# A four-layer graph network on one core: a new order of the work of a turn, a third adjacency buffer, an earlier pause of the gather

## The chip, the cores and the metric

One core of a Trainium2 chip. The metric is the time on the device, in microseconds (us), of one execution of the whole program. The engines are TensorE (PE, with its weight loads PEld), VectorE (DVE), ScalarE (ACT), GpSimd (POOL) and SyncE (SP), which here only issues transfers. Each runs its own list of instructions in order, and they meet at semaphores.

## The reference

Sixteen graphs of 1024 nodes with 64 features (`x`), and for each a 0/1 adjacency matrix with about four ones in a row. Four layers, each with a residual:

```
def ln(x): return (x - mean(x)) / sqrt(var(x) + 1e-5)      # over the 64 features
# layer 0: normalized adjacency with self loops
h = max(ln(x), 0); A1 = adj + I; d = rowsum(A1) ** -0.5
x = x + relu((d[:, None] * A1 * d[None, :]) @ (h @ K0))
# layer 1: three powers of the normalized adjacency
h = max(ln(x), 0); g = A1 * d'[:, None] * d'[None, :]
x = x + concat([h, g h, g g h, g g g h]) @ W.T + b
# layer 2: neighbourhood quantiles
h = max(ln(x), 0)
#   rows with more than 10 neighbours lose every skip-th of them (both directions)
#   agg = 0.25 * q25 + 0.5 * q50 + 0.25 * q75 over the neighbours left and the node itself, per feature
x = x + mlp(h + agg) * mask            # 64 -> 128 -> relu -> 64
# layer 3
h = max(ln(x), 0)
x = x + adj @ (h @ W3) + b3
```

## The kernel before

A *batch* is one graph: 1024 nodes as 8 tiles (`T`) of 128 partitions. The program runs 20 *turns*, and in each it works on up to five batches at once, in the roles `n` (the next), `b` (this), `p` (the last), `c` (two back) and `d` (three back):

- `n`: its adjacency is loaded tile by tile into `adj_f` (`RING` = 2 buffers of 512 KB) and cast to f16 by ScalarE, which sums the degrees on the way (`cast`, L498); `degrees` (L1146) makes the scales; norm0 is computed and split into two bf16 parts (`split`, L1020) for layer 0.
- `b`: TensorE transposes the adjacency (`transpose_adjacency`, L596), then come layer 0 (`h0`, product `lin0`), norm1, and layer 1 as three rounds of an adjacency product `turned_half` (L622), a copy by ScalarE, a product back `turned_back` (L645) and `propagate` on VectorE (L1252): `lin1`, `v1`, `v2`, `v3`, ended by `layer1_out` (L1258). Beside this it prepares the quantiles: nodes with 8 or more in their row are *wide*; `place_of` (PE, L657) and `select_wide` (DVE, L1157) give each a place, `compact` (L674) gathers their rows, `widest` (L1133) and `wide_drops` (L1168) choose what is dropped, `row_keys` (PE, L710, a product per tile) and `row_list` (DVE, L1211, a top 8) list the neighbours of every row, `wide_lists` and `flag_crowds` mend what is special. `row_numbers` (L1215) turns the lists into row numbers for the gather, and `store_h2` (SP) stores the normalized rows to a table in HBM.
- `p`: `weights` (L1220) makes the quantile weights from the lists. It runs at the start of the turn after its lists.
- between the turns: the `gather` (POOL, L400) takes 72 indirect transfers of 128 rows for a batch. It starts when the row numbers are ready and runs on into the next turn. It has pauses, `abreast` (L423), in which it waits for a product or a transposition of the batch behind: after 14 transfers for `lin0`, then for `select`, `lin1`, `v1`, `v2`. For the last batch there is none.
- `c`: VectorE sorts the gathered slots (`sort_1` to `sort_6`, L1036 to L1065), merges the wide ones (`merge_first`, `merge_rest`, `wide_sum`), weighs and sums (`narrow_weighing`, `narrow_sum`, `aggregate`, L1270); TensorE transposes the aggregate and runs the two-layer MLP (`hidden_rows`, L734, ScalarE's `hidden`, L516, `mlp_rows`, L804); `add_mlp` (L1277); then norm3 and layer 3 (`h3`, `lin3`).
- `d`: `add_layer3` (L1264) adds layer 3, and SP stores the result (`store_result`); behind that store on SP stand the load of the next `x` and of tiles 2 to 7 of the next adjacency.

What sets the order: each engine has its turn written out by hand, in the loops `for turn in turns` (SP L326, POOL L448, ScalarE L521, TensorE L813, VectorE L1283). The PSUM banks are used in turn: `ps_tr` has two for transpositions and adjacency products, `ps_key` two for the key products, `ps_prod` and `ps_misc` one each. The tables `TR`, `KEY`, `MISC`, `PROD`, `PARTS` (L79 to L88) number their uses in the order of the turn, and each user waits until the use before its own (two before, where there are two banks) is free. A normalization is four steps: sums on VectorE (`norm_begin`), squares and a root on ScalarE (`norm_spread`), scales on VectorE (`norm_scale`), the result on ScalarE (`norm_apply`).

Of the kernel before, what the change touches and what calls it, by code (L numbers as in the profile page):

```python
# [48 lines left out]
def gnn_stack(nc, x_in, adj, nodemask, w_l0, w_l1, b_l1, w1, b1, w2, b2, w_l3, b_l3, out):  # L49
# [6 lines left out]
    T = N // P  # L56
# [5 lines left out]
    RING = 2  # L62
# [12 lines left out]
    for i in range(-1, B + 3):  # L75
        turns.append({role: (i + ahead if 0 <= i + ahead < B else None)
                      for role, ahead in (("n", 1), ("b", 0), ("p", -1), ("c", -2), ("d", -3))})
# [3 lines left out]
                     ("b", "v1.1"), ("b", "v2.0"), ("b", "v2.1"), ("c", "agg.0"), ("c", "agg.1"), ("b", "v3.0"),  # L81
                     ("b", "v3.1"), ("c", "h3.0"), ("c", "h3.1")])
    KEY = numbered(turns, [("b", "place"), ("b", "compact"), ("b", "pairs"), ("b", "row0"), ("b", "row1"),
                           ("b", "cross"), ("b", "row2"), ("b", "over")] + [("b", f"row{t}") for t in range(3, T)])
# [6 lines left out]
    with ctx:  # L91
# [255 lines left out]
        def _(pool):  # L347
# [52 lines left out]
            def gather(g):  # L400
# [26 lines left out]
                for t in range(T):  # L427
                    if t == 2:
                        abreast(prod_full, PROD.get(("lin0", g + 1), 0) + 1)
# [24 lines left out]
        def _(act):  # L454
# [66 lines left out]
            for turn in turns:  # L521
# [7 lines left out]
                if b is not None:  # L529
                    for t in range(T):  # L530
                        adjacency_columns(b, t)
                    halves("h0", b, columns_t[:, :])
                casts(0, 1)
                if b is not None:
                    norm_spread("norm1", b, h_rows[:, :, 0:C])
# [5 lines left out]
                casts(2, 6)  # L541
                if b is not None:
                    half_of("v1", b, 0, columns_t[:, :])
                casts(6, 7)
                if b is not None:
                    half_of("v1", b, 1, columns_t[:, :])
                casts(7, 8)
                if n is not None:
                    degree_roots(n)
                if b is not None:  # L550
                    halves("v2", b, columns_t[:, :])
                if c is not None:
                    halves("agg", c, columns_t[0:C, :])
                    hidden(c, 0)
                if b is not None:
                    half_of("v3", b, 0, columns_t[:, :])
                if c is not None:
                    hidden(c, 1)
                if b is not None:
                    half_of("v3", b, 1, columns_t[:, :])  # L560
                if b is not None:
                    norm_spread("norm2", b, tiles(h2[b % 2]))
                if n is not None:
                    norm_spread("norm0", n, y)
                if b is not None:
                    norm_apply("norm2", b, tiles(h2[b % 2]), h2_ready)
                    own_rows(b)
                if c is not None:
# [9 lines left out]
        def _(pe):  # L578
# [234 lines left out]
            for turn in turns:  # L813
                b, c = [turn[role] for role in "bc"]
                if b is not None:
                    place_of(b)
# [25 lines left out]
                if c is not None:  # L842
                    spread_wide(c)
                if b is not None:
# [5 lines left out]
                if c is not None:  # L850
                    transpose_features("agg", c, lambda t: agg[:, t, :], C, agg_ready)
                if b is not None:
                    own_weights("v3", b, DEPTH - 3)
# [540 lines left out]
```

## Time and profile before

| | us |
|---|---|
| median of 3 runs | 2063.82 |
| lowest and highest of them | 2052.77, 2066.84 |
| span of the profiled execution | 2057.6 |
| busy in it: VectorE | 1476.0 (72%) |
| TensorE | 1414.9 (69%) |
| POOL | 1277.9 (62%) |
| ScalarE | 811.7 (39%) |

The profiled execution is known by its span, first to last instruction; it lies 6.2 us (0.3%) under the median of the runs. Times in the profile count from the start of the span. Busy shares are averages over the whole of it: at either end stand stretches in which only some of the roles have a batch. A wait line says which engine waited, at which line and tile, and which instruction released it.

### The profile page before, as it was taken

What the parts mean: (1) busy time and instruction counts of PE and PEld (TensorE: products, weight loads), DVE (VectorE), ACT (ScalarE), POOL (GpSimd) and SP (SyncE); (2) the same over time, 40 slices, a digit from 0 to 9 for tenths busy, and PEclk for the clock granted to TensorE, in tenths of its full rate; (3) what the DMA queues carried; (4) which work ended last, traced back from release to release, by engine and by line L of the source; (5) the groups of instructions that cost most, each with busy time, mean ns of one, the idle gap of its engine ahead of it and who ended that gap; (6) DMA issues with size and microseconds to landing.
All of it is one profiled execution on the core that took longest, in us unless ns stands there. A gap on an engine that the chain in (4) does not pass through costs nothing.

```text
span 2057.6 us, 25735 instructions
## 1 busy us (share of the span) xinstructions
PE 1414.9 (69%) x8885; PEld 820.3 (40%) x8997; DVE 1476.0 (72%) x2315; ACT 811.7 (39%) x2292; POOL 1277.9 (62%) x1196
## 2 busy tenths in 40 slices
PE   1778776777868677786967676787867678683314
PEld 0444434444434443443444444444444344342102
DVE  1162886878778686867868697877868687887563
ACT  4443435435343534425253444424353443412101
POOL 2017787766757576575757667574767667577720
PEclk9898878877888888888888888788888788886555
DMA  3113334333233333332333333323333332213210
GB/s 118 62 37 88 55 82 56 86 48 79 36 63 75 57 83 49 90 25 61 75 55 83 50 90 50 79 37 60 77 57 81 48 90 30 23 25 33 25 14 5
DMA packets 106621, 120.22 MB, mean 58 GB/s; under 512 B 71486, under 2 KB 71614, under 8 KB 106430
## 3 DMA queue, kind: packets, MB, share of 16 engines
q0 software_dynamic: 36864, 37.82, 18.5%
q1 hardware_dynamic: 69566, 79.98, 12.4%
q8 instruction: 103, 1.69, 0.3%
q14 instruction: 88, 0.72, 0.1%
HBM read 109.27 MB, written 8.45 MB: 57 GB/s over the span
## 4 chain that ended last, share of the span: by engine, by line
DVE 40%; PE 32%; POOL 11%; issue 9%; ACT 6%; DMA 1%; DVEq 1%; POOLq 0%; SPq 0%; ACTq 0%
PE ps_tr L630 11%; POOL slots L407 10%; DVE lists L1212 6%; PE ps_tr L638 5%; DVE slots L1031 4%; DVE slots L1032 4%; PE ps_prod L649 3%; DVE slots L1114 3%; PE ps_misc L809 2%; PE ps_tr L619 2%; ACT z_mid L494 2%; DVE stat_norm L1007 2%; PE ps_misc L738 2%; ACT adj_t L465 2%; DVE slots L1039 2%
## 5 line engine op out<-in xcount | busy, mean ns | idle before, releaser
L407 POOL DMA_INDIRECT slots<-h_rows,row_no x1152 | 1266.1, 1099 | 687.3 <-issue 341.4
L465 ACT ACTIVATE columns_t<-ps_tr 128x512 f32<-128x512 f32 (+1 forms) x192 | 112.9, 595 | 689.8 <-PE ps_tr L638 518.9
L630 PE MATMUL ps_tr<-adj_t,y_mid 128*128 128x512 bf16 x960 | 259.8, 414 | 24.5 <-DVEq L1025 17.7
L1212 DVE MAX8 lists<-ps_key 128x8 f16<-128x1024 f32 x128 | 157.8, 1232 | 72.7 <-PE ps_key L719 60.7
L503 ACT ACTIVATE adj_n<-adj_f 128x1024 f16<-128x1024 f32 x128 | 134.6, 1052 | 155.9 <-PE ps_key L683 79.3
L630 PEld LDWEIGHTS ps_tr<-adj_t,y_mid 128*128 128x128 bf16 x1024 | 98.6, 105 | 225.5 <-issue 153.6
L630 PE MATMUL ps_tr<-adj_t,z_mid 128*128 128x512 bf16 x240 | 86.7, 512 | 115.2 <-DVEq L1025 114.5
L638 PE MATMUL ps_tr<-adj_t,low 128*64 128x512 bf16 x1024 | 142.3, 402 | 0.0
L484 ACT ACTIVATE h<-x,stat_norm 128x64 f32<-128x64 f32 x256 | 85.1, 334 | 126.7 <-DVEq L1009 126.7
L715 PE MATMUL ps_key<-select_t,dropped 128*128 128x512 bf16 x224 | 90.9, 483 | 63.5 <-DVEq L1144 55.7
L465 ACT ACTIVATE adj_t<-ps_tr 128x1024 bf16<-128x1024 f16 x128 | 119.2, 1032 | 30.6 <-PE ps_tr L602 30.6
L619 PE MATMUL ps_tr<-h_t,w_l_sb 65*128 65x512 f32 x192 | 127.8, 801 | 3.4 <-ACT columns_t L465 3.4
L1031 DVE TENSOR_TENSOR slots<-slots 128x2560 f32<-128x2560 f32 (+1 forms) x64 | 116.8, 1825 | 5.3
L1032 DVE TENSOR_TENSOR slots<-slots 128x2560 f32<-128x2560 f32 (+1 forms) x64 | 116.3, 1817 | 0.0
L494 ACT ACTIVATE h<-x,stat_norm 128x64 f32<-128x64 f32 x256 | 88.2, 427 | 49.0 <-DVEq L1018 49.0
L602 PE MATMUL ps_tr<-ident_h,adj_n 128*128 128x128 f16 x1024 | 78.0, 224 | 42.3 <-ACT adj_t L465 42.3
L1254 DVE TENSOR_TENSOR y_mid<-ps_prod,scales 128x512 f32<-128x512 f32 x48 | 33.2, 691 | 95.1 <-PE ps_prod L649 69.6
L719 PE MATMUL ps_key<-key_diag,adj_t 128*128 128x128 f16 x1024 | 100.7, 256 | 0.0
L649 PEld LDWEIGHTS ps_prod<-both_ident,columns_t 128*128 128x128 f32 x768 | 94.5, 196 | 15.3 <-issue 15.3
L612 PE MATMUL ps_tr<-ident_f,h 128*65 128x128 f32 x128 | 31.1, 423 | 92.7 <-ACT h L494 92.7
L649 PE MATMUL ps_prod<-both_ident,columns_t 128*128 128x64 f32 x768 | 94.2, 277 | 0.0
L719 PEld LDWEIGHTS ps_key<-key_diag,adj_t 128*128 128x128 bf16 x1024 | 83.4, 119 | 23.6 <-issue 14.9
(211 smaller groups left out, 2604.2 us busy)
## 6 DMA issues: line engine op xcount, KB each, us to landing
adj_f<-in_adj SPq DMA_DIRECT2D x128, 512.0 KB, 4.5
slots<-h_rows,row_no POOLq DMA_INDIRECT x1152, 3.3
x<-in_x SPq DMA_DIRECT2D x16, 256.0 KB
h_rows<-h SPq DMA_DIRECT2D x16, 256.0 KB, 4.7
out<-x SPq DMA_DIRECT2D x16, 256.0 KB, 2.7
xc<-in_L_gnn_W SPq DMA_DIRECT2D x1, 64.0 KB
w_sb<-in_L_gnn_W SPq DMA_DIRECT2D x2, 32.0 KB
h_rows<-zeros SPq DMA_DIRECT2D x2, 32.0 KB, 1.5
```

The lines of the kernel that those rows point to most:

```text
L407: pool.indirect_dma_start(out=slots[:, slot_of(par, s), t * C:(t + 1) * C], out_offset=None, in_=table[par][:, :], in_offset=bass.Indirect ...
L465: act.activation(dst, view, ACT.Copy, scale=scale).then_inc(tr_free, 1)
L494: last = act.activation(to[:, t, :], x[g % 4][:, t * C:(t + 1) * C], ACT.Relu, bias=shift[:, t:t + 1], scale=rstd[:, t:t + 1])
L503: act.activation(adj_n[:, t * N:(t + 1) * N], adj_f[:, k % RING, :], ACT.Copy, accum_out=deg[:, t:t + 1]).then_inc(cast_done, 1)
L619: nc.tensor.matmul(tr_bank(f"{name}.{i}", g)[:, :], w_l1_sb[:, part, :], h1_t[:, i * HALF:(i + 1) * HALF], start=True, stop=False)
L630: nc.tensor.matmul(dst[:, :], top_halves(pair_of)[:, j, :], adj_t[g % 3][:, columns[j]], start=(j == 0 and not begun), stop=False)
L638: last = nc.tensor.matmul(dst[rows, :], low_of[:, j, 0:C], adj_t[g % 3][:, columns[j]], start=False, stop=(j >= T - 2))
L649: last = nc.tensor.matmul(ps_prod[:, t * C:(t + 1) * C], columns_t[:, t * P:(t + 1) * P], weights[:, :], start=start, stop=(start or t == ...
L719: last = nc.tensor.matmul(dst[:, j * P:(j + 1) * P], adj_t[g % 3][:, j * N + t * P:j * N + (t + 1) * P], key_diag[:, j, :], start=False, s ...
L1031: st.done(v.tensor_tensor(low_to, first, second, ALU.min))
L1032: step(v.tensor_tensor(high_to, first, second, ALU.max))
L1212: step(v.max(out=lists[:, t * SLOTS:(t + 1) * SLOTS], in_=read_key(f"row{t}", g)))
```

## The change

Nothing is computed otherwise; what is moved is the place of the work in a turn.

- `RING` goes from 2 to 3: three adjacency buffers.
- POOL: the first pause of the gather, after 14 transfers, waits for the last adjacency transposition of the batch behind (`adj7`) and no longer for its `lin0` product.
- `degrees` moves behind the row lists; `place_of` and `select_wide` are done for the next batch at the end of a turn, ahead of layer 3, and not for this batch at its start. `weights` moves from the start of the next turn to the end of the same one; the role `p` is gone.
- VectorE: the sorts open the turn, `add_layer3` follows `sort_2`; `widest` and `wide_drops` stand ahead of the result of `v1`, the first two lists ahead of that of `v2`, `wide_lists` and the third behind it, and the narrow sums and `aggregate` move from ahead of `v2` to behind it, ahead of `layer1_out`. The sums of norm0 stand ahead of the degrees.
- TensorE: row keys 0 and 1 ahead of `v2`, `cross` and row key 2 ahead of `v3`; the transposition of the aggregate and the hidden layer move behind `v3`, with the other row keys among them.
- ScalarE: the spread of norm1 ahead of the first cast; six casts have other places; the hidden layer behind the spread of norm2, the spread of norm0 behind norm2's result and the copy of its rows.

```diff
@@ -61,3 +61,3 @@
     EPS = 1e-5
-    RING = 2
+    RING = 3
     COLS = T + 2
@@ -80,6 +80,7 @@
                   + [("b", "h0.0"), ("b", "h0.1"), ("b", "select"), ("b", "h1.0"), ("b", "h1.1"), ("b", "v1.0"),
-                     ("b", "v1.1"), ("b", "v2.0"), ("b", "v2.1"), ("c", "agg.0"), ("c", "agg.1"), ("b", "v3.0"),
-                     ("b", "v3.1"), ("c", "h3.0"), ("c", "h3.1")])
-    KEY = numbered(turns, [("b", "place"), ("b", "compact"), ("b", "pairs"), ("b", "row0"), ("b", "row1"),
-                           ("b", "cross"), ("b", "row2"), ("b", "over")] + [("b", f"row{t}") for t in range(3, T)])
+                     ("b", "v1.1"), ("b", "v2.0"), ("b", "v2.1"), ("b", "v3.0"), ("b", "v3.1"), ("c", "agg.0"),
+                     ("c", "agg.1"), ("c", "h3.0"), ("c", "h3.1")])
+    KEY = numbered(turns, [("b", "compact"), ("b", "pairs"), ("b", "row0"), ("b", "row1"), ("b", "cross"),
+                           ("b", "row2"), ("b", "over")] + [("b", f"row{t}") for t in range(3, T)]
+                   + [("n", "place")])
     MISC = numbered(turns, [("c", "spread"), ("c", "hid.0"), ("c", "hid.1"), ("c", "mlp")])
@@ -428,3 +429,3 @@
                     if t == 2:
-                        abreast(prod_full, PROD.get(("lin0", g + 1), 0) + 1)
+                        abreast(tr_full, TR.get((f"adj{T - 1}", g + 1), 0) + 1)
                     if t == 4:
@@ -532,5 +533,5 @@
                     halves("h0", b, columns_t[:, :])
+                    norm_spread("norm1", b, h_rows[:, :, 0:C])
                 casts(0, 1)
                 if b is not None:
-                    norm_spread("norm1", b, h_rows[:, :, 0:C])
                     from_tr("select", b, select_t[b % 3][:, :], tr_bank("select", b)[:, :].bitcast(bf16), PAD)
@@ -540,9 +541,9 @@
                     halves("h1", b, h1_t[:, :])
-                casts(2, 6)
+                casts(2, 4)
                 if b is not None:
                     half_of("v1", b, 0, columns_t[:, :])
-                casts(6, 7)
+                casts(4, 5)
                 if b is not None:
                     half_of("v1", b, 1, columns_t[:, :])
-                casts(7, 8)
+                casts(5, 8)
                 if n is not None:
@@ -551,18 +552,15 @@
                     halves("v2", b, columns_t[:, :])
+                    halves("v3", b, columns_t[:, :])
                 if c is not None:
                     halves("agg", c, columns_t[0:C, :])
-                    hidden(c, 0)
                 if b is not None:
-                    half_of("v3", b, 0, columns_t[:, :])
+                    norm_spread("norm2", b, tiles(h2[b % 2]))
                 if c is not None:
+                    hidden(c, 0)
                     hidden(c, 1)
                 if b is not None:
-                    half_of("v3", b, 1, columns_t[:, :])
-                if b is not None:
-                    norm_spread("norm2", b, tiles(h2[b % 2]))
-                if n is not None:
-                    norm_spread("norm0", n, y)
-                if b is not None:
                     norm_apply("norm2", b, tiles(h2[b % 2]), h2_ready)
                     own_rows(b)
+                if n is not None:
+                    norm_spread("norm0", n, y)
                 if c is not None:
@@ -813,5 +811,4 @@
             for turn in turns:
-                b, c = [turn[role] for role in "bc"]
+                n, b, c = [turn[role] for role in "nbc"]
                 if b is not None:
-                    place_of(b)
                     transpose_adjacency(b)
@@ -841,5 +838,5 @@
                     turned_back("v1", "v1", b, both_ident, False)
-                if c is not None:
-                    spread_wide(c)
-                if b is not None:
+                    pe.wait_ge(dropped_ready, b + 1)
+                    row_keys(b, 0)
+                    row_keys(b, 1)
                     own_weights("v2", b, DEPTH - 2)
@@ -850,5 +847,15 @@
                 if c is not None:
-                    transpose_features("agg", c, lambda t: agg[:, t, :], C, agg_ready)
+                    spread_wide(c)
                 if b is not None:
+                    cross_drops(b)
                     own_weights("v3", b, DEPTH - 3)
+                    row_keys(b, 2)
+                    for i in range(2):
+                        turned_half("v3", b, i, y_mid, low, begun=True)
+                    loop_rows("v3", b)
+                    turned_back("v3", "v3", b, both_ident, False)
+                if c is not None:
+                    transpose_features("agg", c, lambda t: agg[:, t, :], C, agg_ready)
+                if b is not None:
+                    count_over(b)
                 if c is not None:
@@ -856,3 +863,3 @@
                 if b is not None:
-                    turned_half("v3", b, 0, y_mid, low, begun=True)
+                    row_keys(b, 3)
                 if c is not None:
@@ -860,12 +867,3 @@
                 if b is not None:
-                    turned_half("v3", b, 1, y_mid, low, begun=True)
-                    loop_rows("v3", b)
-                    pe.wait_ge(dropped_ready, b + 1)
-                    row_keys(b, 0)
-                    row_keys(b, 1)
-                    turned_back("v3", "v3", b, both_ident, False)
-                    cross_drops(b)
-                    row_keys(b, 2)
-                    count_over(b)
-                    row_keys(b, 3)
+                    row_keys(b, 4)
                 if c is not None:
@@ -873,6 +871,6 @@
                 if b is not None:
-                    row_keys(b, 4)
-                    row_keys(b, 5)
-                    row_keys(b, 6)
-                    row_keys(b, 7)
+                    for t in range(5, T):
+                        row_keys(b, t)
+                if n is not None:
+                    place_of(n)
                 if c is not None:
@@ -1283,3 +1281,3 @@
             for turn in turns:
-                n, b, p, c, d = [turn[role] for role in "nbpcd"]
+                n, b, c, d = [turn[role] for role in "nbcd"]
                 st.restart()
@@ -1291,8 +1289,2 @@
 
-                if p is not None:
-                    weights(p)
-                if b is not None:
-                    select_wide(b)
-                if d is not None:
-                    add_layer3(d)
                 if c is not None:
@@ -1304,3 +1296,7 @@
                     sort_2(c)
+                if d is not None:
+                    add_layer3(d)
+                if c is not None:
                     sort_3(c)
+                    sort_4(c)
                 if b is not None:
@@ -1309,8 +1305,7 @@
                 if c is not None:
-                    sort_4(c)
+                    sort_5(c)
                 if b is not None:
-                    norm_scale("norm1", b, s_root)
                     wide_keys(b)
+                    norm_scale("norm1", b, s_root)
                 if c is not None:
-                    sort_5(c)
                     sort_6(c)
@@ -1321,2 +1316,5 @@
                     propagate(b, "lin1")
+                    widest(listed[:, :], key_w[:, :], key_left)
+                    wide_drops(b)
+                    propagate(b, "v1")
                 if c is not None:
@@ -1324,4 +1322,7 @@
                     wide_sum(c)
+                row_lists(0, 2)
                 if b is not None:
-                    propagate(b, "v1")
+                    propagate(b, "v2")
+                    wide_lists(b)
+                row_lists(2, 3)
                 if c is not None:
@@ -1331,11 +1332,6 @@
                 if b is not None:
-                    propagate(b, "v2")
-                    widest(listed[:, :], key_w[:, :], key_left)
-                    wide_drops(b)
-                if n is not None:
-                    degrees(n)
-                row_lists(0, 2)
-                if b is not None:
                     layer1_out(b)
                     norm_begin("norm2", b)
+                    flag_crowds(b)
+                row_lists(3, 4)
                 if n is not None:
@@ -1344,9 +1340,4 @@
                 if b is not None:
-                    wide_lists(b)
-                row_lists(2, 3)
-                if b is not None:
-                    flag_crowds(b)
-                row_lists(3, 4)
-                if b is not None:
                     norm_scale("norm2", b)
+                row_lists(4, 5)
                 if c is not None:
@@ -1354,5 +1345,9 @@
                     norm_begin("norm3", c)
+                row_lists(5, 8)
+                if b is not None:
+                    row_numbers(b)
                 if n is not None:
+                    degrees(n)
                     norm_scale("norm0", n, d0[n % 2])
-                row_lists(4, 8)
+                    select_wide(n)
                 if c is not None:
@@ -1360,3 +1355,3 @@
                 if b is not None:
-                    row_numbers(b)
+                    weights(b)
                 if c is not None:
```

## Rows read from the trace of the kernel before

**Rows 1.** VectorE's timeline (start, duration), row numbers and first sort.

```profile
141.44 0.20 DVE L1217 TENSOR_SCALAR row_no<-row_no_f 128x81 int32<-128x81 f32 x1
...
234.26 0.20 DVE L1217 TENSOR_SCALAR row_no<-row_no_f 128x81 int32<-128x81 f32 x1
...
241.68 2.83 DVE L1039 TENSOR_TENSOR slots<-slots 128x2560 f32<-128x2560 f32 x1 [0.40 <-DMA slots<-h_rows,row_no]
...
1865.22 0.22 DVE L1217 TENSOR_SCALAR row_no<-row_no_f 128x81 int32<-128x81 f32 x1
```

**Rows 2.** Waits (total, times, longest), one turn, 950.9 to 1067.4.

```profile
POOL slots L407 <- PE ps_prod L649: 10.4, 1, 10.4
...
PE ps_key L707 <- DVEq L1200: 4.2, 1, 4.2
...
DVE place L1158 <- PE ps_key L663: 3.6, 1, 3.6
...
DVE lists L1212 <- PE ps_key L719: 2.6, 2, 1.8
DVE y_mid L1254 <- PE ps_prod L649: 2.4, 1, 2.4
DVE z_mid L1279 <- PE ps_misc L809: 2.4, 1, 2.4
...
DVE z_mid L1023 <- ACT z_mid L494: 2.3, 1, 2.3
```

**Rows 3.** VectorE's timeline of one turn; in brackets the idle time before.

```profile
940.79 0.17 DVE L1221 TENSOR_SCALAR scale<-wide 128x8 f32<-128x8 bf16 x1 [0.25 <-DVE low L1024]
...
950.94 2.83 DVE L1039 TENSOR_TENSOR slots<-slots 128x2560 f32<-128x2560 f32 x1 [0.34 <-DVE x L1266]
...
965.06 0.69 DVE L1248 SCALAR_TENSOR_TENSOR y_mid<-ps_prod,scales 128x512 f32<-128x512 f32 x1
...
972.11 1.49 DVE L1055 TENSOR_TENSOR slots<-slots 128x1280 f32<-128x1280 f32 x1
...
985.90 0.69 DVE L1254 TENSOR_TENSOR y_mid<-ps_prod,scales 128x512 f32<-128x512 f32 x1 [1.03 <-issue]
```

**Rows 4.** ScalarE's waits in the first 45 us (total, times, longest).

```profile
ACT adj_n L503 <- DMA adj_f<-in_adj: 9.7, 6, 2.8
ACT y_mid L484 <- DVEq L1009: 2.0, 1, 2.0
```

**Rows 5.** TensorE's timeline of the same turn.

```profile
962.71 2.00 PE L649 MATMUL ps_prod<-w_l_sb,columns_t 128*128 128x64 f32 x16
...
979.87 3.68 PE L834 MATMUL ps_prod<-w_l_sb,h_t 65*128 65x64 f32 x16 [0.68 <-ACT h_t L465]
...
988.74 3.19 PE L630 MATMUL ps_tr<-adj_t,y_mid 128*128 128x512 bf16 x7 [1.68 <-DVEq L1025]
```

**Rows 6.** ScalarE's timeline of the same turn.

```profile
968.71 1.06 ACT L503 ACTIVATE adj_n<-adj_f 128x1024 f16<-128x1024 f32 x1 [5.29 <-PE ps_key L683]
...
1030.00 0.35 ACT L484 ACTIVATE h<-x,stat_norm 128x64 f32<-128x64 f32 x1 [6.95 <-DVEq L1009]
```

**Rows 7.** TensorE's timeline of turn 0, first seven products of v1.

```profile
86.33 2.87 PE L630 MATMUL ps_tr<-adj_t,y_mid 128*128 128x512 bf16 x7 [0.22 <-issue]
```

**Rows 8.** TensorE by stretches: length, busy (instructions), granted clock, DMA share, GB/s.

```profile
977.20:983.50 6.30, 5.57 (x25) 0.50 0.55 170
...
1036.50:1040.60 4.10, 4.10 (x19) 0.50 0.16 24
```

**Rows 9.** TensorE's timeline of the last turn: hidden layer and MLP.

```profile
2026.04 2.04 PE L738 MATMUL ps_misc<-columns_t,w_sb 64*128 64x512 f32 x2 [0.87 <-ACT merged L518]
...
2029.40 3.68 PE L809 MATMUL ps_misc<-w_sb,merged 128*128 128x64 f32 x16
```

**Rows 10.** POOL's timeline: first gathers of batches 0 and 1.

```profile
142.63 1.59 POOL L407 DMA_INDIRECT slots<-h_rows,row_no  x1 [127.11 <-DVEq L1218]
...
236.15 0.94 POOL L407 DMA_INDIRECT slots<-h_rows,row_no  x1 [1.98 <-DMA h_rows<-h]
```

More of the change, by code:

```diff
@@ L551, in _ @@
                     halves("v2", b, columns_t[:, :])
+                    halves("v3", b, columns_t[:, :])
                 if c is not None:
                     halves("agg", c, columns_t[0:C, :])
-                    hidden(c, 0)
-                if b is not None:
-                    half_of("v3", b, 0, columns_t[:, :])
-                if c is not None:
-                    hidden(c, 1)
-                if b is not None:
-                    half_of("v3", b, 1, columns_t[:, :])
                 if b is not None:
                     norm_spread("norm2", b, tiles(h2[b % 2]))
-                if n is not None:
-                    norm_spread("norm0", n, y)
+                if c is not None:
+                    hidden(c, 0)
+                    hidden(c, 1)
                 if b is not None:
@@ L841, in _ @@
                     turned_back("v1", "v1", b, both_ident, False)
-                if c is not None:
-                    spread_wide(c)
-                if b is not None:
+                    pe.wait_ge(dropped_ready, b + 1)
+                    row_keys(b, 0)
+                    row_keys(b, 1)
                     own_weights("v2", b, DEPTH - 2)
@@ L850, in _ @@
                 if c is not None:
+                    spread_wide(c)
+                if b is not None:
+                    cross_drops(b)
+                    own_weights("v3", b, DEPTH - 3)
+                    row_keys(b, 2)
[4 more added lines that the diff above has]
+                if c is not None:
                     transpose_features("agg", c, lambda t: agg[:, t, :], C, agg_ready)
                 if b is not None:
-                    own_weights("v3", b, DEPTH - 3)
+                    count_over(b)
                 if c is not None:
@@ L1304, in _ @@
                     sort_2(c)
+                if d is not None:
+                    add_layer3(d)
+                if c is not None:
                     sort_3(c)
+                    sort_4(c)
                 if b is not None:
@@ L1309, in _ @@
                 if c is not None:
-                    sort_4(c)
+                    sort_5(c)
                 if b is not None:
+                    wide_keys(b)
                     norm_scale("norm1", b, s_root)
-                    wide_keys(b)
                 if c is not None:
-                    sort_5(c)
                     sort_6(c)
```

## The prediction

> **What bounds the kernel now.** I read three things in this order: the start of each turn on VectorE, the waits within one turn, and the timelines of VectorE, TensorE and ScalarE beside each other. The row numbers of batch 1 are ready at 234.46 us and those of batch 15 at 1865.44 [rows 1]; between them lie 14 turns, so a turn takes 116.5. The head up to the first sort (241.68) and the tail behind the last row numbers (2057.6 - 1865.4 = 192.2) are the rest. In the turn that starts at 940.79 no engine is full: VectorE waits 3.6 for the places, 2.6 for row keys, 2.4 for the v1 product, 2.4 for the MLP, 2.3 for z, 1.0 on "issue", and about 2.5 in small pieces, some 16.8 with the places at this turn's own 3.9 [rows 2, 3]. So its work is 116.7 - 16.8 = 99.9 a turn. The gather is not behind: POOL waits 10.4 for the lin0 product in a turn, and it ends before the next row numbers [rows 2]. The bound is the ping-pong between VectorE, TensorE and ScalarE. The change removes no work in a turn; what counts is which waits are left.
>
> **The pause and the third buffer.** The last adjacency transposition ends about 10 us before the lin0 product, so up to 10.4 us of pause go [rows 2]. Those gathers then run beside the sorts. Nobody waits for them in a steady turn, so I take 0 for the turn; the price for POOL is in the rivals. Three buffers hide ScalarE's waits for adjacency; in the first turn these are 9.7 in six [rows 4]. Between 0 and -9.7 I take -3, since two transfers in flight already follow each other at 2.6 us.
>
> **A steady turn, wait by wait** (0 is the restart behind the last split).
> 1. Places and weights: select moves ahead of the split, behind the place product, which now stands on TensorE behind the row keys: its wait of 3.6 to 3.9 goes. The 3.6 of weights and 1.7 of selection move into the stretch in which ScalarE normalizes; the 2.3 wait for z goes too, the one for y stays at 0.5.
> 2. lin0 product: it ends at 964.71 (962.71 + 2.00 [rows 5]), 23.9 behind the restart. h3 now starts 0.5 later against the restart, so 24.2. Work ahead of its reader: sorts 1 to 3, 14.1 (950.94 to 965.06), sort 4, four passes of 1.49, and the output of layer 3, 1.0 [rows 3]: 21.1. **New wait 3.1.** The result store and, behind it on SP, the loads of x and of tiles 3 to 7 come 2.6 later; the first cast comes at 30, so nobody waits. ScalarE's spread for norm1 no longer stands behind the cast, which in the trace waits 5.3 for the compaction and starts 1.2 behind the mean [rows 6].
> 3. lin1: in the trace from the mean (967.5) to its end (979.87 + 3.68) 16.05 [rows 5], now 14.85. VectorE's work between (sort 5, wide keys, scale, sort 6, merge) is 11.3. **New wait 3.5** (it covers the 1.03 of "issue" [rows 3]).
> 4. v1: its own weights are done 3.6 behind lin1 (983.55 to 988.74 less the idle 1.68 [rows 5]), 1.3 behind the parts, so TensorE does not idle. With idle 1.68 the first seven matmuls took 3.19, with 0.22 2.87 in turn 0 [rows 5, 7], and the whole of v1 9.5 instead of 10.5. Against this stand 9.1 of list and drop work. **New wait 1.7** (was 2.4).
> 5. v2 and v3: two row keys (1.9) and own weights (1.95) stand in front of v2, cross and row 2 in front of v3. VectorE has 11.4 of merging, wide sum and two lists against 3.85 + 8.2 behind the parts: 0 (slack 0.8). The narrow sum covers v3.
> 6. Here the change costs. The aggregate now ends after v3, so TensorE idles 4.6 (v3 done to aggregate), about as long as the 4.2 before the count in the trace [rows 2], behind which its row keys and the MLP ran at 1.2 GHz: granted clock 0.50 [rows 8]. Behind the aggregate: ScalarE first does layer 1's spread (mean at +2.75, 3.0 long as at 1030.00 [rows 6]), then hidden 0 (0.7), TensorE hidden 1 2.04, row key 4 1.9, MLP 0.5 + 3.68 [rows 9]: together 14.65. VectorE's own work meanwhile: layer 1 out 2.75, flag, row 3, sums for norm0, scale, row 4: 7.4. **New wait 7.25**, in place of 2.6 and 2.4.
> 7. Row key 7 0.6, restart 0.25.
>
> Sum: 3.1 + 3.5 + 1.7 + 7.25 + 0.6 + 0.5 + 0.25 = 16.9, so a turn is 116.8, I take 116.9 against 116.5: **nothing is gained in a steady turn**. At full clock in step 6 (row key and hidden 0.95 and 1.05, MLP 2.4) the chain is 10.9, row key 7 costs nothing, and a turn is 113.3.
>
> **The head.** Row numbers of batch 0 were at 141.64. Buffers -3; the sums of norm0 stand ahead of the degrees, so ScalarE's 2.0 wait goes [rows 4]; the spread ahead of the cast -1.4; list and drop work (9.1) and three lists leave the chain behind v2 for TensorE's time, less two waits of 1 for row keys, -10. Together 125.4. The gather then takes as long as before (142.6 to 234.2 [rows 10]), to 218.0, and the sort starts 5 to 7.5 behind it: 224.5 instead of 241.68. Turn 1 alone would end at 221: row numbers 86.6 behind the first (92.8 before, -11.4, +5.2 since ScalarE's transposed columns now wait behind its norm0), and 8.6. In the first full turn TensorE is ahead, and the 3.1 of step 2 drop out. Head: -17.2 - 3 = **-20**.
>
> **The tail.** Output of layer 3 for batch 14 stood in the wait for the last gather, now behind sort 2: +1.0. Nothing else in it moves.
>
> **Sum.** 224.5 + 14 x 116.9 - 11.0 (row numbers to first sort) - 3.1 + 192.2 + 1.0 = 2040 against the profiled 2057.6. That span is 6.2 below the median of 2063.82 and inside the runs' 2052.77 to 2066.84, so 2046.
>
> **Rivals.**
> - *Full clock behind the aggregate.* TensorE is busy almost all of the 14.6, and a turn is 113.3: 14 x 3.6 = 50 less, 1996. Against it: from 977.2 to 983.5, busy for 5.6 of 6.3, the clock stays at 0.50, and in the MLP of the trace, with row keys on both sides, too [rows 8].
>  The Trainium skill (TensorE: Matmul & The Clock Gate, "What's actually happening") says that what warms the clock up is sustained busy time and not a number of matmuls; by that rule this rival's 1996 would come true, and the two stretches just named disagree.
> - *Low clock on into h3 and lin0 (slower).* Place: TensorE's wait between row key 7 and h3, 6.95 before, about 10 now, since weights and selection stand ahead of z's split. Price: h3's second half 2.9 and its product 1.9 at 1.2 GHz, straight into the wait for lin0, which is open. A turn is then 121.7 and the kernel 2046 + 67 = 2113. It decides from 1.3 us a turn on (18 of head gain over 14 turns). Against it: in the tail h3 follows 11.0 of idling and costs about 4.6 for its first half, as in every turn.
> - *The head does not move*, because the gather or the landing holds the first sort, or ScalarE's order eats the gain: then 2064, no change.
> - *POOL becomes the bound.* Gathers beside sorts 1 and 2 take about 2.5 instead of 0.94. Ten of those are 15 us, in place of the 10.4 pause: POOL then needs 106 a turn, still below 116.9, so this alone changes nothing; it only cuts off gains below 106.
>
> **Chances.** My forecast (a turn of 115.5 to 118.5, its own range 2026 to 2068) 0.52, of which 0.20 below 2043 and 0.32 within 1%; full or partly full clock (1990 to 2020) 0.23; low clock further on, or another slip of over 2.7 us a turn, 0.15, 0.04 of it within 1%; unmoved head 0.10, half of it within 1%, half beyond. Within 1% is what a measurement of this kernel can tell from no change: 2043 to 2084. So faster 0.43, same 0.41, slower 0.16. The range leaves out the ends of both rivals: 1994 to 2085.
>
> **What would show it.** Right: first sort at 220 to 228; a period of 116 to 118; VectorE's longest wait in a turn at the MLP or row 4 (together 7), then lin1 and lin0 with 3 to 4; no wait for places; POOL's pause under 2 us; clock 0.50 from the aggregate to row key 6. Wrong: no low clock there (period 113), a lin0 wait above 6 (period 120 and more), a POOL that starts its gather late, or the first sort still near 241.

## The result, and the profile after

| | before | after |
|---|---|---|
| median of 4 runs | 2062.26 | 2082.26 |
| lowest and highest | 2052.77, 2066.84 | 2080.52, 2083.51 |
| profiled execution | 2057.6 | 2078.8 |
| VectorE busy in it | 1476.0 | 1475.7 |
| TensorE busy | 1414.9 | 1461.2 |
| POOL busy | 1277.9 | 1364.0 |

The ratio to the kernel before is 1.0106, 95% interval 1.0078 to 1.0134: the change costs 1%, 20 us. The forecast was 2046, a gain of 18. The range up to 2085 holds 2082 near its end, and not by the forecast's own working.

VectorE's timeline (start, duration) gives the stages, as [rows 1] did:

```profile
122.67 0.20 DVE L1215 TENSOR_SCALAR row_no<-row_no_f 128x81 int32<-128x81 f32 x1
...
211.31 0.20 DVE L1215 TENSOR_SCALAR row_no<-row_no_f 128x81 int32<-128x81 f32 x1
...
225.45 2.83 DVE L1037 TENSOR_TENSOR slots<-slots 128x2560 f32<-128x2560 f32 x1 [5.32 <-DMA slots<-h_rows,row_no]
...
1884.67 0.20 DVE L1215 TENSOR_SCALAR row_no<-row_no_f 128x81 int32<-128x81 f32 x1
```

The row numbers of batch 1 come at 211.51 and not at 234.46: the head gives back 23 (16 at the first sort, which now waits 5.3 for the last gather and waited 0.4 [rows 1]). Between batches 1 and 15 lie 1673.4 and not 1631.0, so a turn takes 119.5 on average where it took 116.5: 42 lost. The tail is 193.9 (2078.8 - 1884.87) against 192.2. -23 + 42 + 2 = +21, the difference of the spans.

VectorE's waits (total, times, longest) in one turn, 1179.5 to 1299.2, against [rows 2]:

```profile
DVE y_mid L1246 <- PE ps_prod L647: 5.7, 1, 5.7
DVE lists L1210 <- PE ps_key L717: 4.8, 2, 3.2
DVE y_mid L1252 <- PE ps_prod L831: 3.6, 1, 3.6
DVE z_mid L1277 <- PE ps_misc L807: 2.9, 1, 2.9
DVE y_mid L1252 <- PE ps_prod L647: 2.0, 1, 2.0
```

The places are gone from the list, as is the wait for z. First stands the wait for the lin0 product (L1246), with 5.7 where 3.1 was forecast.

TensorE's timeline of the same turn (h3 at 1177.77 and 1181.27, h0 from 1196.34, lin0 at 1204.23, then the chain behind the aggregate), then its stretches (length, busy with instructions, granted clock, DMA share, GB/s):

```profile
1168.96 0.19 PE L659 MATMUL ps_key<-wide,prefix 128*128 128x8 bf16 x1 [2.57 <-DVEq L1150]
...
1177.77 3.57 PE L628 MATMUL ps_tr<-adj_t,z_mid 128*128 128x512 bf16 x8 [8.43 <-DVEq L1023]
1181.27 1.66 PE L636 MATMUL ps_tr<-adj_t,low_z 128*64 128x512 bf16 x8
...
1196.34 0.31 PE L632 MATMUL ps_tr<-ident_b,y_mid 128*128 128x128 bf16 x1 [1.51 <-ACT adj_t L466]
...
1197.19 2.86 PE L628 MATMUL ps_tr<-adj_t,y_mid 128*128 128x512 bf16 x7
...
1204.23 2.00 PE L647 MATMUL ps_prod<-w_l_sb,columns_t 128*128 128x64 f32 x16
...
1266.41 1.89 PE L610 MATMUL ps_tr<-ident_f,z_mid 128*64 128x128 f32 x8 [4.47 <-DVEq L1273]
...
1277.15 3.67 PE L807 MATMUL ps_misc<-w_sb,merged 128*128 128x64 f32 x16
```

```profile
1177.90:1187.60 9.70, 9.65 (x47) 0.76 0.12 14
1195.60:1206.60 11.00, 10.26 (x66) 0.84 0.32 48
...
1266.40:1276.60 10.20, 9.37 (x34) 0.50 0.38 26
1276.60:1280.70 4.10, 4.10 (x19) 0.50 0.95 20
```

And what answers to the first two stretches in the kernel before, its h3 and its h0 to lin0:

```profile
1170.42 3.57 PE L630 MATMUL ps_tr<-adj_t,z_mid 128*128 128x512 bf16 x8 [6.59 <-DVEq L1025]
1173.92 1.16 PE L638 MATMUL ps_tr<-adj_t,low_z 128*64 128x512 bf16 x8
...
1188.63 0.22 PE L634 MATMUL ps_tr<-ident_b,y_mid 128*128 128x128 bf16 x1 [1.44 <-ACT adj_t L465]
...
1189.07 1.67 PE L630 MATMUL ps_tr<-adj_t,y_mid 128*128 128x512 bf16 x7
```

```profile
1170.30:1180.10 9.80, 9.63 (x53) 0.80 0.21 26
1188.20:1197.20 9.00, 8.57 (x66) 1.00 0.04 7
```

TensorE starts h3 after an idle 8.43, with another 2.57 shortly before it (before: 6.59 in one). Its clock over h3 is 0.76 instead of 0.80, and over h0 and lin0 0.84 instead of 1.00: the first seven products of h0 take 2.86, in the kernel before 1.67. The last two stretches are step 6: the whole chain behind the aggregate stays at 0.50, at 1.2 GHz, as forecast.

POOL's waits in that turn (total, times, longest), and its group of gathers in the page (busy, mean ns, idle before):

```profile
POOL slots L408 <- DVEq L1216: 11.5, 1, 11.5
```

```profile
L408 POOL DMA_INDIRECT slots<-h_rows,row_no x1152 | 1352.2, 1174 | 621.1 <-issue 339.8
```

The pause of 10.4 [rows 2] is gone and POOL now waits 11.5 for the row numbers: it is not behind.

### The profile page after: what moved, and what is told of

Read it like the earlier page. It is cut to its first block, busy times and chain, and to the rows that moved or that the text cites. A ratio compares the mean times of both kernels' runs of the same rounds, so it can differ in the third digit from the quotient of the medians.

```text
span 2078.8 us, 25753 instructions
## 1 busy us (share of the span) xinstructions
PE 1461.2 (70%) x8888; PEld 848.0 (41%) x8997; DVE 1475.7 (71%) x2315; ACT 806.0 (39%) x2292; POOL 1364.0 (66%) x1196
## 4 chain that ended last, share of the span: by engine, by line
PE 38%; DVE 32%; ACT 13%; POOL 8%; issue 7%; DMA 1%; DVEq 0%; POOLq 0%; SPq 0%; ACTq 0%
PE ps_tr L628 10%; POOL slots L408 7%; DVE lists L1210 5%; ACT adj_t L466 5%; PE ps_tr L636 5%; PE ps_prod L647 4%; ACT h L485 3%; DVE slots L1112 3%; PE ps_tr L610 3%; PE ps_tr L617 3%; PE ps_prod L831 3%; PE ps_misc L807 3%; ACT h L495 2%; PE ps_misc L736 2%; DVE slots L1124 1%
## 5 line engine op out<-in xcount | busy, mean ns | idle before, releaser
L408 POOL DMA_INDIRECT slots<-h_rows,row_no x1152 | 1352.2, 1174 | 621.1 <-issue 339.8
L628 PE MATMUL ps_tr<-adj_t,y_mid 128*128 128x512 bf16 x992 | 276.3, 425 | 16.3 <-DVEq L1023 12.8
L628 PEld LDWEIGHTS ps_tr<-adj_t,y_mid 128*128 128x128 bf16 x1024 | 104.2, 108 | 204.2 <-issue 135.6
L636 PE MATMUL ps_tr<-adj_t,low 128*64 128x512 bf16 x1024 | 136.6, 389 | 0.0
L466 ACT ACTIVATE adj_t<-ps_tr 128x1024 bf16<-128x1024 f16 x128 | 119.9, 1032 | 29.7 <-PE ps_tr L600 29.7
L617 PE MATMUL ps_tr<-h_t,w_l_sb 65*128 65x512 f32 x192 | 121.6, 767 | 0.0
L485 ACT ACTIVATE h<-x,stat_norm 128x64 f32<-128x64 f32 x256 | 85.4, 335 | 86.1 <-DVEq L1007 86.1
L717 PE MATMUL ps_key<-key_diag,adj_t 128*128 128x128 f16 x1024 | 105.9, 265 | 0.0
L628 PEld LDWEIGHTS ps_tr<-adj_t,z_mid 128*128 128x128 bf16 x256 | 27.7, 118 | 187.3 <-issue 176.1
L717 PEld LDWEIGHTS ps_key<-key_diag,adj_t 128*128 128x128 bf16 x1024 | 87.9, 124 | 25.2 <-issue 17.9
L600 PEld LDWEIGHTS ps_tr<-ident_h,adj_n 128*128 128x128 f16 x1024 | 66.2, 104 | 58.7 <-issue 57.4
```

The lines of the kernel that those rows point to most:

```text
L408: pool.indirect_dma_start(out=slots[:, slot_of(par, s), t * C:(t + 1) * C], out_offset=None, in_=table[par][:, :], in_offset=bass.Indirect ...
L466: act.activation(dst, view, ACT.Copy, scale=scale).then_inc(tr_free, 1)
L485: last = act.activation(scratch[:, t, :], x[g % 4][:, t * C:(t + 1) * C], ACT.Square, bias=less_mean[:, t:t + 1], accum_out=var[:, t:t + 1])
L600: last = nc.tensor.transpose(view[:, j, :], adj_n[:, t * N + j * P:t * N + (j + 1) * P], ident_h[:, :])
L617: nc.tensor.matmul(tr_bank(f"{name}.{i}", g)[:, :], w_l1_sb[:, part, :], h1_t[:, i * HALF:(i + 1) * HALF], start=True, stop=False)
L628: nc.tensor.matmul(dst[:, :], top_halves(pair_of)[:, j, :], adj_t[g % 3][:, columns[j]], start=(j == 0 and not begun), stop=False)
```

## The experiments

*Theory A*: the turn is longer because TensorE's clock is low in h3 and h0, just ahead of the one wait that is open there. *Theory B*: without its pause the gather runs beside h3, h0 and lin0 and slows them. Each run was taken in three rounds beside the kernel before; the period T is the distance of the row numbers of batches 1 and 15 over 14, as above. The last column is read from TensorE's timelines: in 13 turns h3 and h0 both run, and it counts those in which h0, from its first product to the start of lin0, took 7.6 us or more, where the others take 6.3 to 6.5. Most kernels carry a helper which gives TensorE products whose result the next true product overwrites:

```diff
+            def keep_busy(name, g, times):
+                tr_turn(name, g)
+                for k in range(times):
+                    nc.tensor.matmul(tr_bank(name, g)[:, :], ones, adj_t[g % 3][:, 0:HALF], start=True, stop=True)
```

| run | built on | median | ratio to before [95%] | T | slow h0, of 13 |
|---|---|---|---|---|---|
| before | | 2062.26 | | 116.5 | 1 |
| after | before | 2082.26 | 1.0106 [1.0078, 1.0134] | 119.5 | 12 |
| busy_h3 | after | 2043.67 | 0.9917 [0.9889, 0.9945] | 116.65 | 1 |
| busy_agg | after | 2079.99 | 1.0094 [1.0061, 1.0127] | 119.2 | 11 |
| pause_lin0 | after | 2087.24 | 1.0121 [1.0092, 1.0150] | 119.8 | 13 |
| late_weights | after | 2048.99 | 0.9930 [0.9906, 0.9955] | 117.2 | 4 |
| hidden_first | after | 2068.89 | 1.0042 [1.0021, 1.0063] | 118.3 | 8 |
| chain_warm | busy_agg | 2001.21 | 0.9719 [0.9679, 0.9758] | 113.9 | 3 |
| late_chain | chain_warm | 1984.58 | 0.9641 [0.9602, 0.9680] | 112.75 | 8 |
| select_in_wait | late_chain | 1981.68 | 0.9602 [0.9571, 0.9634] | 112.5 | 9 |
| two_buffers | after | 2087.49 | 1.0143 [1.0107, 1.0178] | 119.55 | 13 |
| before_busy | before | 2050.54 | 0.9949 [0.9926, 0.9973] | 116.45 | 0 |

**busy_h3**: the two idle stretches ahead of h3 are filled.

```diff
+                if c is not None:
+                    keep_busy("h3.0", c, 10)
                 if n is not None:
                     place_of(n)
                 if c is not None:
+                    keep_busy("h3.0", c, 30)
                     turned_half("h3", c, 0, z_mid, low_z)
```

> The changed kernel, with 10 products of 128x512 bf16 more before the place product and 30 more behind it, into the bank that the first half of h3 overwrites; all else as in the changed kernel. Theory A (the longer wait of TensorE ahead of h3 lowers its clock in h3 and h0, and that makes the lin0 product 2.6 us later than I had it): the granted clock from h3 to lin0 is near 1.00 in place of 0.77 and 0.84, VectorE's wait for lin0 falls from 5.7 to about 2.5 us, a turn from 119.5 to 116.3, and the median from 2082 to about 2037. Theory B (lin0 is late for another reason: the gathers that now run beside the transpositions and h0, or ScalarE's copies): the clock rises, but the wait stays above 5 and the time at 2082.

TensorE's timeline of a turn (h3's first half, h0's first half), then VectorE's at the reader of lin0:

```profile
921.99 1.89 PE L628 MATMUL ps_tr<-adj_t,z_mid 128*128 128x512 bf16 x8 [1.72 <-DVEq L1031]
...
938.65 1.67 PE L628 MATMUL ps_tr<-adj_t,y_mid 128*128 128x512 bf16 x7
```

```profile
946.61 0.69 DVE L1254 SCALAR_TENSOR_TENSOR y_mid<-ps_prod,scales 128x512 f32<-128x512 f32 x1 [1.52 <-PE ps_prod L647]
```

The first products of h3 take 1.89 instead of 3.57, those of h0 1.67, and VectorE waits 1.52 for lin0 instead of 5.7. Nothing but the fillers was added, and 38.6 are gone. Theory A is shown: the low clock there is worth more than the whole loss. It is worth more because the fillers also raise the clock in h3, which was low in the kernel before too (0.80).

**pause_lin0**: the gather's pause as before.

```diff
-                        abreast(tr_full, TR.get((f"adj{T - 1}", g + 1), 0) + 1)
+                        abreast(prod_full, PROD.get(("lin0", g + 1), 0) + 1)
```

> The changed kernel, with the gather's first pause back at the lin0 product. Theory A: POOL's pause is some 10 us a turn again, POOL still ends ahead of the next row numbers, and the time stays at 2082 within 5. Theory B (gathers beside the transpositions and h0 make lin0 late): VectorE's wait for lin0 falls by 2 to 3 us, a turn to 117, the median to about 2047.

POOL's waits over the span, then VectorE's wait for lin0 in the turn 1067 to 1186.7:

```profile
POOL slots L408 <- PE ps_prod L647: 154.3, 17, 12.4
```

```profile
DVE y_mid L1246 <- PE ps_prod L647: 5.7, 1, 5.7
```

The pause is back and the wait is 5.7 as in the change: theory B falls. The earlier pause is neither the loss nor a gain beyond the noise (the intervals of this and of the change overlap).

**busy_agg**: the wait for the aggregate is filled.

```diff
                 if c is not None:
+                    keep_busy("agg.0", c, 18)
                     transpose_features("agg", c, lambda t: agg[:, t, :], C, agg_ready)
```

> The changed kernel, with 18 products of 128x512 bf16 more in TensorE's 4.5 us wait for the aggregate, into the bank that the aggregate's transposition overwrites. If the low clock behind that wait is what the MLP chain costs, the chain from the aggregate to the MLP falls from 14.5 to about 11 us, VectorE's waits for row 3, row 4 and the MLP from 7.7 to about 4.1, a turn to 116, the median to about 2032. If VectorE then only waits at the next place (lin0), or the clock falls in the chain all the same, the time stays within 10 us of 2082.

TensorE's timeline behind the aggregate of one turn:

```profile
1142.80 1.03 PE L610 MATMUL ps_tr<-ident_f,z_mid 128*64 128x128 f32 x8 [0.57 <-DVEq L1279]
...
1149.10 2.04 PE L736 MATMUL ps_misc<-columns_t,w_sb 64*128 64x512 f32 x2 [2.84 <-ACT merged L519]
```

The transposition runs at full clock (1.03 for eight, 1.89 after). Then TensorE waits 2.84 for ScalarE's `hidden`, which stands behind the spread of norm2, and the second half of the hidden layer and the MLP take 2.04 and 3.67 again. The fill was in the right place, but a second gap behind it undoes it.

**late_weights**: `weights` and `select_wide` go back from the end of the turn to the start of the next, on VectorE alone.

```diff
                 st.restart()
...
+                if p is not None:
+                    weights(p)
+                if b is not None:
+                    select_wide(b)
...
                     norm_scale("norm0", n, d0[n % 2])
-                    select_wide(n)
...
-                if b is not None:
-                    weights(b)
                 if c is not None:
                     dve.wait_ge(z_ready, c + 1)
```

> The changed kernel, with the weights and the selection on VectorE back at the start of the next turn, behind the two splits (5.3 us). Theory A: the split of z, and with it h3, comes 2.9 us earlier behind the row numbers, TensorE's wait ahead of h3 falls from 11 to 8 us, the two steps lie in the wait for lin0 (5.7), which shrinks to under 1; a turn falls by 1.8 us to 117.7, the median to about 2057. If the end of the turn is bound by ScalarE's two normalizations instead, the time stays at 2082 or grows by up to 2.4 us a turn (2115).

TensorE's timeline of a turn and of h0 in the next one, and VectorE's at lin0 of the first:

```profile
923.43 3.57 PE L628 MATMUL ps_tr<-adj_t,z_mid 128*128 128x512 bf16 x8 [5.88 <-DVEq L1023]
...
942.71 2.69 PE L628 MATMUL ps_tr<-adj_t,y_mid 128*128 128x512 bf16 x7
...
1058.63 1.67 PE L628 MATMUL ps_tr<-adj_t,y_mid 128*128 128x512 bf16 x7
```

```profile
952.37 0.69 DVE L1246 SCALAR_TENSOR_TENSOR y_mid<-ps_prod,scales 128x512 f32<-128x512 f32 x1
```

In the first of these turns the clock in h3 and h0 is as low as after (3.57, 2.69); h0 is that slow in 4 of 13 turns, and in the other 9 it is at full clock, as in the second. VectorE waits for lin0 in neither kind, since it has 5.3 more of other work ahead of its reader. In the changed kernel the two steps stood where VectorE would otherwise wait for z and y; there 2.9 and 1.2 of waiting come back, while the 5.7 in front of lin0 goes. The turn is 2.3 shorter.

**chain_warm** fills the wait for the aggregate and takes the gap behind it away: `hidden(c, 0)` on ScalarE ahead of norm2's spread.

```diff
 # TensorE
+                    keep_busy("agg.0", c, 18)
 # ScalarE
+                if c is not None:
+                    hidden(c, 0)
                 if b is not None:
                     norm_spread("norm2", b, tiles(h2[b % 2]))
                 if c is not None:
-                    hidden(c, 0)
                     hidden(c, 1)
```

> The kernel of busy_agg (18 products more in TensorE's wait for the aggregate), and on ScalarE the copy of hidden 0 ahead of layer 1's spread in place of behind it. Theory A (the chain behind the aggregate is held first by ScalarE's spread, 3 us, and then by the low clock that the wait for it brings): no wait of 2.8 us between hidden 0 and hidden 1, full clock up to the MLP, VectorE's waits for row 3, row 4 and the MLP from 7.7 to 2 to 3 us, a turn from 119.5 to 114.5, the median from 2080 to about 2012. Theory B (other waits take over, or the clock falls anyway): above 2065.

TensorE's timeline of a turn (the hidden layer and the MLP), its stretches (the chain, then h3, then h0), and VectorE at lin0:

```profile
994.38 1.09 PE L737 MATMUL ps_misc<-columns_t,w_sb 64*128 64x512 f32 x2 [0.29 <-issue]
...
1000.12 2.26 PE L808 MATMUL ps_misc<-w_sb,merged 128*128 128x64 f32 x16
```

```profile
994.40:1002.40 8.00, 6.78 (x43) 0.96 0.20 27
906.00:915.00 9.00, 8.50 (x42) 0.80 0.12 13
923.00:932.00 9.00, 7.88 (x61) 1.00 0.33 53
```

```profile
932.53 0.69 DVE L1253 SCALAR_TENSOR_TENSOR y_mid<-ps_prod,scales 128x512 f32<-128x512 f32 x1 [3.33 <-PE ps_prod L648]
```

The chain runs at 0.96, with hidden products of 1.09 and 1.12 and an MLP of 2.26. h3's first half is still slow (3.45, behind an idle 8.46), but h0 runs at full clock here and in 10 of 13 turns, and the wait for lin0 is 3.33, near the forecast's 3.1. So an idle stretch of 8.4 ahead of h3 alone does not slow h0. Nor is the gain over busy_agg the chain's alone: averaged over the 13 turns the wait for lin0 falls from 5.4 to 3.9.

**late_chain** is chain_warm with late_weights' edit.

```diff
+                    weights(p)
...
+                    select_wide(b)
...
-                    select_wide(n)
...
-                    weights(b)
```

> chain_warm and late_weights together. If the two places are independent, a turn is 117.3 less 5, about 112.3, and the median about 1981; if the shorter chain only opens the wait for lin0 or lin1 again, between 2010 and 2049.

T is 112.75. The two gains don't add up (113.9 less 2.3 would be 111.6); the likely reason, not tested alone, is that the wait for lin0, into which the moved work goes, was down to 3.9 on average already.

**two_buffers**: the change with two adjacency buffers.

```diff
-    RING = 3
+    RING = 2
```

> The changed kernel with two adjacency buffers in place of three. By my steps the third buffer is worth 3 us in the first turn and nothing later: the median is about 2085, the row numbers of batch 0 near 126 in place of 122.7. If the casts, which stand ahead of ScalarE's copies of v1, wait for adjacency then, a turn grows by 1 to 3 us and the median to 2096 or more.

ScalarE's waits for adjacency in the first 45 us (total, times, longest), with two buffers and after:

```profile
ACT adj_n L504 <- DMA adj_f<-in_adj: 9.2, 6, 2.4
```

```profile
ACT adj_n L504 <- DMA adj_f<-in_adj: 3.5, 4, 1.2
```

The row numbers of batch 0 come at 129.7 and not at 122.9, and the period is that of the change (119.55). But busy_h3 and pause_lin0, which have three buffers and differ from the change only behind that point, have them at 126.7 and 126.1. So the third buffer is worth 3 to 7, in the head, and the medians (2087.49, and 2087.24 for pause_lin0) don't tell even this from noise.

**before_busy**: 28 fillers ahead of h3 in the kernel before.

```diff
                 if c is not None:
+                    keep_busy("h3.0", c, 28)
                     turned_half("h3", c, 0, z_mid, low_z)
```

> The kernel before, with 28 products of 128x512 bf16 more in TensorE's wait of 7 us ahead of h3. They raise the clock in h3 there too, and the lin0 product comes some 2 us earlier; but VectorE reads it behind sort 3 and does not wait for it there, so the time stays at that of the kernel before, within 6 us. If the clock of h3 counts by itself, wherever VectorE waits, it falls by 14 x 2, to about 2035.

TensorE's timeline, h3's first half of one turn:

```profile
932.92 1.89 PE L630 MATMUL ps_tr<-adj_t,z_mid 128*128 128x512 bf16 x8
```

h3 is at full clock, and the period 116.45 against 116.50: VectorE waits for lin0 in none of the 13 turns there. The median is nevertheless 0.5% below, 9 us where at most 6 was expected. The profiled execution is the slowest of this kernel's ten (2057.19, the others 2042.15 to 2054.23), so its period doesn't speak for the median. Whether the higher clock gave these 9 us stays open.

**hidden_first** is the move of ScalarE's in chain_warm without any filler.

```diff
+                if c is not None:
+                    hidden(c, 0)
                 if b is not None:
                     norm_spread("norm2", b, tiles(h2[b % 2]))
                 if c is not None:
-                    hidden(c, 0)
                     hidden(c, 1)
```

> The changed kernel with ScalarE's copy of hidden 0 ahead of layer 1's spread, and no products more. Theory A (the order and the low clock each hold the chain behind the aggregate; taking away one leaves the other): at low clock row key 3 keeps TensorE until 6 us behind the aggregate anyway, hidden 1 starts 0.5 us earlier, a turn falls from 119.5 to about 119, the median to about 2075. Theory B (the order alone is what chain_warm gained): about 2005 to 2020.

The turn is 118.3: the order alone takes off 1.2, the fill alone (busy_agg) 0.3, both together 5.6. With the order alone h0 is slow in 8 of 13 turns and not in 12, and 1.6 of the 5.6 is the shorter wait for lin0 (5.5 on average in the change, 3.9 in chain_warm), so the chain's own share is smaller than 5.6. The lin0 wait stays open, in the waits over the span (total, times, longest):

```profile
DVE y_mid L1247 <- PE ps_prod L648: 96.0, 15, 15.7
```

**select_in_wait** keeps `select_wide` at the end of the turn, behind norm3's scale, where VectorE waits for z.

```diff
-                if b is not None:
-                    select_wide(b)
...
                 if c is not None:
                     norm_scale("norm3", c)
+                if n is not None:
+                    select_wide(n)
```

> late_chain with the selection (1.7 us) not behind the splits but in VectorE's wait for z (2.9 us), behind norm3's scale. That wait falls to 1.2 and nothing else moves: a turn from 112.7 to 111, the median from 1985 to about 1961. If VectorE waits for lin0 instead, which was then ready only just in time, it stays at 1985.

VectorE's waits over the span, late_chain first, then select_in_wait:

```profile
DVE y_mid L1259 <- PE ps_prod L837: 70.7, 16, 10.4
...
DVE z_mid L1028 <- ACT z_mid L495: 46.1, 16, 2.9
...
DVE y_mid L1253 <- PE ps_prod L648: 24.4, 2, 13.9
```

```profile
DVE y_mid L1259 <- PE ps_prod L837: 79.7, 16, 10.4
...
DVE y_mid L1253 <- PE ps_prod L648: 41.3, 11, 17.8
...
DVE z_mid L1028 <- ACT z_mid L495: 24.2, 16, 2.9
```

The waits for z fall by 21.9, those for lin0 and lin1 rise by 16.9 and 9.0, and the spans are equal (1984.3): the wait was moved and not removed. Its median is the lowest of all, but not told apart from late_chain's. Both are 4% faster than the kernel before.

## Why the prediction was wrong

- **Step 2 failed**: the new wait for lin0 was put at 3.1 and is 5.7 in the turn shown (100.8 in 15 waits over the span, one of them 15.7 in the head). It is 2.6 of the 3.2 by which all waits of this turn (20.1) exceed the 16.9 of the forecast. VectorE's work ahead of the reader is 21.0, as forecast (21.1); lin0 ends 26.6 behind the restart (1206.23 less 1179.63, the first sort) and not 24.2:

```profile
1179.63 2.82 DVE L1037 TENSOR_TENSOR slots<-slots 128x2560 f32<-128x2560 f32 x1 [0.35 <-DVE low L1022]
```

 Of these 2.4, about 2.1 are TensorE's durations: h3's second-part products take 1.66 instead of 1.16 (0.5), and from the start of h0 to the end of lin0 it is 9.9 (1196.34 to 1206.23) instead of 8.3, of which the first seven products make 1.2 (2.86 instead of 1.67). The rest is that h3 starts a little later against the restart. I carried over the durations that TensorE had before, while the change opened the wait behind them. busy_h3 shows the clock as the cause: with it up, the wait is 1.5.
- **The slower rival** named this mechanism, its place and the point from which it decides (1.3 a turn), and had 0.15. It priced h3's second half, which stayed at full clock; the price lies in h3's second-part products and in h0. The argument against it was the tail, where h3 follows 11.0 of idling and costs about 4.6 for its first half. The change did lengthen that half (5.1, 1177.77 to 1182.85, against 4.6 in the turn of before shown), and the tail has no h0 behind h3, so it could not answer for h0. The trace of before could have warned: in one of its 13 turns (h3 at 577.90) h0 runs at low clock too, with the same 6.59 of idling ahead of h3, and VectorE waits 1.45 for lin0.
- **Steps 1, 3, 4, 5 and 6 held**: no wait for places, z gone, y 0.3; lin1 3.6 (3.5 forecast); v1 2.0 (1.7); none for v2 and v3; row keys and MLP together 7.7 (7.25), in the waits of the turn.
- **Two slips of the sums**: the waits listed for the kernel before add up to 17.1 and not 16.8, so VectorE's work is 99.6 a turn (it is 99.6 in the change too, 119.7 less 20.1). And with the chain at 10.9 and no wait for row key 7 the listed terms give a turn of 112.5 and not 113.3. Neither touches the step that failed.
- **Full clock behind the aggregate** did not come: from 1266.4 to 1276.6 TensorE is busy for 9.37 of 10.2 and in the 4.1 behind it throughout, at 0.50 all the way. The Trainium skill (TensorE: Matmul & The Clock Gate, "What's actually happening") has the clock rise with sustained busy time whatever is issued; this trace disagrees again, as [rows 8] did. chain_warm shows that the clock, once up at the start of the chain and with no long gap in it, stays up; its turn is 113.9.
- **The head** came as forecast: row numbers of batch 0 at 122.9 (125.4 forecast), first sort at 225.45 (224.5). The buffers' term was -3 and is 3 to 7, the second stage 88.6 long and not 86.6.
- **POOL**: the gathers grew (mean 1099 to 1174 ns), with a wait of 11.5 a turn left, so POOL needs 108 a turn (119.7 less 11.5), where 106 was forecast. As forecast, it binds nothing.
- **The sum**: row numbers of batch 15 were forecast at 1847.0 and came at 1884.9. Of the 37.9, -2.0 lie in the row numbers of batch 1, 0.9 in the first turn and 39.0 in 13 turns of 119.9 instead of 116.9; with 0.7 in the tail this is the 38.6 between 2040.2 and 2078.8.

**Open**: what lets the clock fall in h0. The idle time ahead of h3 doesn't decide it: behind 8.2 to 8.5 us of idling h0 is slow in 12 of 13 turns in the change, 8 in hidden_first and 3 in chain_warm; behind 5.9, in 4 in late_weights and 8 in late_chain. That the change's longer idle stretch (8.4 instead of 6.6) made it fall is therefore not shown; shown is that filling the stretch keeps the clock up. Nor is it known why fill and order are worth so little alone. No run tells either.

## What to carry to other kernels

When a change moves work across a wait, list the waits that it opens and ask of each producer at which clock its duration was read, and over all turns rather than in one: a duration at full clock may not survive another order. Where VectorE waited for what the low clock slowed, filling the idle stretch ahead of it with products nobody reads gave back 2.9 us a turn (busy_h3). In a chain, remove the gaps inside it along with the one ahead, since either alone may give little (0.3 and 1.2 against 5.6, part of it at lin0). And moving work into a wait pays only if it is not taken from in front of another wait that is open.

## What the hardware showed that I had not expected

- 40 products a turn whose results nobody reads took 38.6 off 2082: busy_h3's timeline, 1.89 for what took 3.57.
- A low clock lasts through 14.3 with 13.47 of it busy (1266.4 to 1280.7), while in chain_warm it was up and stayed up over small gaps (6.78 busy of 8.0, 0.96).
- Kernels with the same idle time ahead of h3 differ in how often the clock falls again in the busy stretch behind it (the table's last column).
- A gather's issue on POOL takes 2.42 beside VectorE's sorts of 2560 and 1.23 beside the narrower ones, while VectorE's own 2.82 is unchanged, and the gathers come one to a pass (starts 1183.58, 1186.31 and 1189.17 beside passes from 1182.38, 1185.23 and 1187.97); timelines of POOL (two rows) and VectorE, the kernel after:

```profile
1183.58 2.42 POOL L408 DMA_INDIRECT slots<-h_rows,row_no  x1 [0.30 <-issue]
...
1195.77 1.23 POOL L408 DMA_INDIRECT slots<-h_rows,row_no  x1 [0.30 <-issue]
...
1182.38 2.82 DVE L1038 TENSOR_TENSOR slots<-slots 128x2560 f32<-128x2560 f32 x1
```

 The Trainium skill (SBUF — State Buffer, "Terms") has VectorE and GpSimd share one pair of ports, held for a whole instruction, and the loser blocked. The rows agree for POOL's side only: the sorts of 2560 take 2.81 to 2.90 in the whole trace.
